# A mixture-of-experts stage that keeps a list of tokens: steps gather by token and add into a sum in DRAM

## The chip, the cores and the metric

One core of one Trainium2 chip. The time is the device time of one launch, in microseconds. Names used below: PE is TensorE, DVE is VectorE, ACT is ScalarE, POOL is GpSimd, SP is SyncE. SP and ACT can issue plain DMAs; POOL issues the indirect ones (rows picked by a list of indices).

## What is computed

Cross-attention followed by a feed-forward layer of eight experts, each token going to two of them, everything in float32. Only the second half is touched by the change:

```python
def _L0_ffn_ref(hidden_states, router_w, w1, w2):
    flat = hidden_states.reshape(-1, H)                    # 1792 tokens x 256
    gate_probs = jax.nn.softmax(flat @ router_w, axis=-1)  # 8 experts
    topk_w, topk_idx = jax.lax.top_k(gate_probs, 2)
    topk_w = topk_w / jnp.clip(topk_w.sum(-1, keepdims=True), EPS)
    cw = jnp.zeros((T, E)).at[jnp.arange(T)[:, None], topk_idx].add(topk_w)
    h = jax.nn.silu(jnp.einsum('td,edf->etf', flat, w1))   # 256 -> 512
    y = jnp.einsum('etf,efd->etd', h, w2)                  # 512 -> 256
    out = jnp.einsum('etd,te->td', y, cw)
...
x = x + _L0_xattn_ref(_layernorm(x), ctx_1024, ctx_1024, mask, Wq, bq, Wk, bk, Wv, bv, Wo, bo)
x = x + _L0_ffn_ref(_layernorm(x), router_w, w1, w2)
```

## The kernel before

The attention half runs over 16 batches and ends near 316 us of the span. Then comes the routing: PE projects the attention output (`project_output`), DVE adds it to `x2` (`residual`, line 972), normalises the rows into `xn2` (`normalise_rows`, line 1006), PE makes the logits, DVE finds each token's first and second expert (`find_first`, `find_second`) and PE ranks the tokens of each expert (`rank`, line 1425).

The experts' work is cut into 21 steps (`STEPS`) of 256 rows (`TG`), each step with the weights of one expert. `place_rows` (line 1052) works out for each token and each of its two choices the row it takes in an array that is sorted by expert. The rows themselves are moved:

- SP fills the DRAM array `sorted_x` (5376 x 256) with zeros (line 416), so that rows that belong to no token are harmless.
- POOL scatters the normalised rows into it: 28 indirect DMAs of 128 rows of 1 KB (line 583), 14 tiles of tokens by two choices.
- In each step SP loads 256 consecutive rows of `sorted_x` (`load_block`, line 438) and two weights of 512 KB (`load_w1`, `load_w2`).
- After step 21, POOL gathers the outputs from `sorted_y` back to the tokens' order, 28 indirect DMAs again (line 610), DVE multiplies each by its weight and adds it to `x2` (line 1169), and SP writes `out` in seven parts (line 469).

Every product is made of three: each operand is split into a high part (a cast to float32r) and a low part (what the cast left over). In step t of the loop the engines do, in this order and all double-buffered (`par`):

- PE (`step`, line 1472): `hidden(t)`, 24 products; `rows_transpose(t+1)`, 4 transposes; `expert_out(t-1)`, 24 products.
- ACT (line 777): high part of w1 of t+1 (`w1_high`), the DMA of the output block t-2 to `sorted_y` (`write_block`), high part of the rows t+1 (`rows_high`), and two Silu passes of t (`silu`: the value and its high part).
- DVE (`expert_step`, line 1119): low part of the rows t+1 (`rows_low`), low part of the hidden values of t (`h_low`), copy of the output t-1 out of PSUM (`copy_y`), high part of w2 of t+1 (`w2_high`).
- POOL (line 591): low parts of w1 of t+1 and of w2 of t (`split_low`).

Steps 0 to 2 and 19 and 20 are written out, those between run in a loop of two steps a turn (`Fori`). The order is that of the program; nothing reorders it. A wait on a semaphore holds all that stands behind it on the same engine.

## Time and profile before

| | |
|---|---|
| runs, us | 590.64, 589.96, 587.99; median 589.96 |
| the profiled execution, us | 589.78, its span 588.0 |
| busy: PE, DVE, ACT, POOL | 435.2, 376.6, 231.5, 264.1 us |
| granted TensorE clock, mean over the span | 0.877 |
| attention with its start | 0 to 316 us |
| output projection, routing, ranking | 316 to 363 us |
| POOL's scatter of the rows | 363 to 400 us |
| first row block to last output | 400 to 544 us |
| gather, weighted sum, write | 545 to 588 us |

The span runs from the first to the last instruction of the profiled execution; 1.8 us of its own time lie around it. The stages are read off the timelines and the chain that ended last. A matmul's row lasts longer than the distance to the next one, since they are pipelined: distances between starts are the measure. Indirect DMAs stand under POOL with the time in which POOL makes them; their landing is a different number, in the view of the DMA issues.

### The profile page before, as it was taken

Reading aid. Unit: us, or ns where it says so; the run is one execution under the profiler, and the core shown is the slowest. Engines: PE = TensorE matmul, PEld = TensorE weight load, DVE = VectorE, ACT = ScalarE, POOL = GpSimd, SP = SyncE. Lnnn points to the kernel's source line nnn. Section 1 sums busy time; section 2 is a strip of 40 time slices with the busy share of each in tenths; the row PEclk is TensorE's granted clock in tenths of the full one; section 3 lists DMA queues with packets and bytes.
Section 4 is the critical chain, followed back from the end, with each engine's and each line's share of the span. In section 5 each row is a group of like instructions: output and inputs, shape, how many; then the busy total and the mean of one; then the engine's idle time right before and its main releaser. Section 6 shows DMA issues by size and latency. Waiting matters only on the chain.

```text
span 588.0 us, 10921 instructions
## 1 busy us (share of the span) xinstructions
PE 435.2 (74%) x4123; PEld 384.7 (65%) x4123; DVE 376.6 (64%) x749; ACT 231.5 (39%) x296; POOL 264.1 (45%) x170
## 2 busy tenths in 40 slices
PE   2657799999999999999987482004999999998000
PEld 2546588888888888878766472003999999998000
DVE  3765647777777777777734856001899999997233
ACT  3321245555555555555552030001645554552000
POOL 7352412222221122222004202775699899895574
PEclk9886679999999999999998775555999999999655
DMA  7979499999899998997443700525588787862354
GB/s 190 182 192 256 151 136 142 139 130 141 142 139 144 143 140 142 141 142 104 48 129 118 258 1 33 200 107 180 165 261 245 243 258 233 254 213 90 107 155 130
DMA packets 82025, 93.00 MB, mean 158 GB/s; under 512 B 19345, under 2 KB 74801, under 8 KB 81985
## 3 DMA queue, kind: packets, MB, share of 16 engines
q1 hardware_dynamic: 73584, 79.60, 63.1%
q0 software_dynamic: 2688, 7.34, 4.0%
q10 hardware_dynamic: 5712, 5.51, 2.8%
q8 instruction: 27, 0.44, 0.4%
q14 instruction: 14, 0.11, 0.1%
HBM read 51.58 MB, written 22.14 MB: 125 GB/s over the span
## 4 chain that ended last, share of the span: by engine, by line
PE 44%; issue 16%; DVE 16%; POOL 9%; ACT 8%; DMA 3%; ACTq 2%; DVEq 0%; POOLq 0%; SPq 0%
PE ps L1182 17%; PE ps L1232 9%; PE ps L1248 7%; PE ps L1262 5%; POOL sorted_x L583 4%; POOL chosen_rows L610 4%; DVE neg_max L839 4%; ACT h_hi L771 3%; ACT h_f L770 2%; DVE y_out L1116 2%; DVE k_f L823 2%; ACTq L775 1%; PE ps L1275 1%; DVE h_lo L1109 1%; ACT probs L660 1%
## 5 line engine op out<-in xcount | busy, mean ns | idle before, releaser
L839 DVE TENSOR_REDUCE neg_max<-ps 112x1 f32<-112x376 f32 x256 | 133.0, 546 | 48.1 <-PE ps L1232 44.4
L588 POOL TENSOR_TENSOR w_lo<-w_raw,w_hi 128x1024 fp32r<-128x1024 f32 x42 | 117.8, 2826 | 24.0 <-DVE w_hi L1105 14.3
L660 ACT ACTIVATE probs<-ps 125x1344 f32<-125x1344 f32 x64 | 82.8, 1293 | 59.0 <-PE ps L1248 56.3
L1232 PE MATMUL ps<-k_stack,q_stack 98*112 98x376 f32 x256 | 90.5, 396 | 10.3 <-issue 5.2
L498 POOL TENSOR_TENSOR k_lo<-k_f,k_hi 128x752 fp32r<-128x752 f32 x16 | 28.7, 1791 | 87.4 <-ACT k_hi L634 84.8
L489 POOL TENSOR_TENSOR ctx_lo<-ctx_raw,ctx_hi 128x752 fp32r<-128x752 f32 x16 | 28.8, 1798 | 80.3 <-ACT ctx_hi L627 80.3
L1232 PEld LDWEIGHTS ps<-k_stack,q_stack 98*112 98x112 f32 x256 | 43.0, 182 | 27.5 <-DVE neg_max L839 21.3
L1109 DVE TENSOR_TENSOR h_lo<-h_f,h_hi 128x1024 fp32r<-128x1024 f32 x21 | 52.6, 2503 | 11.1 <-ACT h_hi L771 11.1
L1248 PE MATMUL ps<-q_stack,k_stack 100*125 100x224 f32 x384 | 54.8, 279 | 2.1 <-ACT probs L660 2.1
L1248 PEld LDWEIGHTS ps<-q_stack,k_stack 100*125 100x125 f32 x384 | 51.2, 193 | 2.8 <-ACT probs L660 1.8
L1182 PE MATMUL ps<-flat_t_hi,w_hi 128*128 128x256 f32 x168 | 50.4, 300 | 3.3 <-DVE flat_t_lo L1098 3.2
L1262 PE MATMUL ps<-probs,v_wide 125*32 125x112 f32 x1536 | 50.2, 264 | 0.7 <-ACT probs L660 0.7
L1182 PE MATMUL ps<-w_hi,h_hi 128*128 128x256 f32 x168 | 49.2, 293 | 1.9 <-DVE h_lo L1109 1.9
L754 ACT CAST flat_t_hi<-ps 128x512 fp32r<-128x512 f32 x21 | 12.3, 587 | 94.5 <-PE ps L1443 94.5
L1182 PE MATMUL ps<-flat_t_hi,w_lo 128*128 128x256 f32 x168 | 48.1, 286 | 0.0
L1182 PE MATMUL ps<-flat_t_lo,w_hi 128*128 128x256 f32 x168 | 48.0, 286 | 0.0
L1182 PE MATMUL ps<-w_lo,h_hi 128*128 128x256 f32 x168 | 47.4, 282 | 0.0
L1182 PE MATMUL ps<-w_hi,h_lo 128*128 128x256 f32 x168 | 47.4, 282 | 0.0
L583 POOL DMA_INDIRECT sorted_x<-xn,place x28 | 27.2, 971 | 44.5 <-DVE place L1071 36.3
L1443 PE MATMUL ps<-ident,rows 128*128 128x128 f32 x84 | 13.1, 280 | 43.6 <-DMA rows<-sorted_x 43.6
L1105 DVE CAST w_hi<-w_raw 128x1024 fp32r<-128x1024 f32 x21 | 45.3, 2156 | 0.0
L1262 PEld LDWEIGHTS ps<-probs,v_wide 125*32 125x32 f32 x1536 | 34.8, 110 | 13.2 <-issue 11.8
(169 smaller groups left out, 990.0 us busy)
## 6 DMA issues: line engine op xcount, KB each, us to landing
w_raw<-w SPq DMA_DIRECT2D x42, 512.0 KB, 3.8
k_stack<-k_hi SPq DMA_DIRECT2D x64, 188.0 KB, 6.1
k_stack<-k_lo SPq DMA_DIRECT2D x32, 188.0 KB, 8.9
ctx_raw<-ctx_t SPq DMA_DIRECT2D x32, 187.5 KB, 8.3
q_stack<-q_scratch SPq DMA_DIRECT2D x32, 168.0 KB
sorted_x<-zeros SPq DMA_DIRECT2D x1, 5376.0 KB, 17.5
rows<-sorted_x SPq DMA_DIRECT2D x21, 256.0 KB, 3.9
sorted_y<-y_out ACTq DMA_DIRECT2D x21, 256.0 KB, 2.9
```

The costliest lines, as they stand in the source:

```text
L489: pool.tensor_tensor(cl[b.par][:, :, :], c_raw[b.par][:, :, :], ch[b.par][:, :, :].bitcast(F32), ALU.subtract).then_inc(cl_ready, 1)
L498: pool.tensor_tensor(kl[:, :, :], kf[:, :, :], kh[:, :, :].bitcast(F32), ALU.subtract)\
L583: pool.indirect_dma_start(sorted_x, bass.IndirectOffsetOnAxis(ap=place[c][:, n:n + 1], axis=0), xn2[:, n, :], None).then_inc(scattered, 16)
L588: pool.tensor_tensor(low[t.par][:, :, :], raw[:, :, :], high[t.par][:, :, :].bitcast(F32), ALU.subtract).then_inc(done, 1)
L660: act.activation(pf[j % 2][:, :, :], ps[0:CT, BK_ST:BK_ST + KT, 0:4 * S], ACT.Exp).then_inc(pf_ready, 1)
L839: dve.tensor_reduce(neg_max[:, s:s + 1], ps[0:S, BK_MAX + s % 2, 0:CP], AX.X, ALU.max, negate=True).then_inc(max_read, 1)
L1105: dve.tensor_copy(w2h[t.par][:, :, :], w_raw[t.par][1][:, :, :]).then_inc(w2h_ready, 1)
L1109: dve.tensor_tensor(hl[t.par][:, :, :], hf[t.par][:, :, :], hh[t.par][:, :, :].bitcast(F32), ALU.subtract).then_inc(hl_ready, 1)
L1182: last = pe.matmul(o, lhs, rhs, start=n == 0, stop=n == len(terms) - 1)
L1232: pe.matmul(ps[0:S, BK_MAX + a, 0:CP], qs[b.ring][0:R_MAX, q, S * a:S * (a + 1)], ks[b.ring][0:R_MAX, q, :], start=True, stop=True).then_i ...
L1248: last = pe.matmul(ps[0:CT, BK_ST + k3, 2 * S * q:2 * S * (q + 1)], ks[b.ring][0:ROWS, 2 * j + q, k3 * CT:(k3 + 1) * CT], qs[b.ring][0:ROW ...
L1262: last = pe.matmul(ps[VC * i:VC * (i + 1), BK_OUT, S * j:S * (j + 1)], vx[b.par][:, k3, 2 * j + i // 2 + HALF * (i % 2), :], pf[j % 2][:, ...
```

## The change

Not the rows are sorted, but a list of pairs (token, weight). What it does, by engine; line numbers of the changed kernel are those of this section only:

- **The list.** POOL makes two small tables early on: `no_row` (pairs for rows that belong to no token: the token number is T..T+255, a spare row, and the weight 0) and the token numbers of `of_token` (lines 555 to 558). SP writes `no_row` to `sorted_rows` (5376 x 2) during the first turn of the attention. `weigh` stands ahead of `place_rows` on DVE, and puts the weights into `of_token`. POOL then scatters the pairs, 28 indirect DMAs of 128 pairs of 8 bytes. SP loads the list back (`load_rows_of`, line 452): the pairs of steps 0 and 1 first, then those of the 19 others, each step with two pairs a partition.
- **Inputs.** SP writes `xn2` to `xn_rows` and `x2` to `total`, seven parts each, with 256 spare rows of zeros. The zero fill of `sorted_x` is gone.
- **Steps.** POOL gathers the rows of step t+2 by token, two indirect DMAs (`gather_rows`, line 599), and then adds the output of step t-1 into `total`, two indirect DMAs with an addition (`add_rows`, line 611). Each `add_rows` waits until the one before has landed. No step is written by ACT, and none loaded by SP.
- **Weights.** The low parts of w1 and w2 go from POOL to DVE, the high part of w2 from DVE to ACT (`w2_high`, line 787). DVE multiplies the output by the weight of its row as it takes it out of PSUM (`weigh_y`, line 1124), two instructions of 128 x 256 in place of one copy of 128 x 512.
- **End.** The gather, the weighted sum on DVE and the seven writes are gone. SP waits for the last addition and copies `total` to `out`, DRAM to DRAM, in one DMA of 1792 KB.
- All 21 steps are written out on every engine, without a loop. Two mask tables of the attention share space with `probs`.

```diff
@@ gpsimd @@
+            pool.memset(no_row[:, :, :, 1], 0.0)
+            pool.iota(no_row[:, :, :, 0].bitcast(I32), pattern=[[0, STEPS], [1, 2]], base=T, channel_multiplier=2)\
+                .then_inc(tokens_set, 1)
...
             pool.wait_ge(placed, 1)
-            pool.wait_ge(zero_rows, 16)
+            pool.wait_ge(weights_ready, 1)
+            pool.wait_ge(rows_cleared, 16)
             for n in range(NT):
                 for c in range(TOP):
-                    pool.indirect_dma_start(sorted_x, bass.IndirectOffsetOnAxis(ap=place[c][:, n:n + 1], axis=0),
-                                            xn2[:, n, :], None).then_inc(scattered, 16)
+                    pool.indirect_dma_start(sorted_rows, bass.IndirectOffsetOnAxis(ap=place[c][:, n:n + 1], axis=0),
+                                            of_token[:, n, c, :], None).then_inc(scattered, 16)
+            def token_of(t, a):
+                return bass.IndirectOffsetOnAxis(ap=of_row[:, t.n, a, 0:1].bitcast(I32), axis=0)
+            def gather_rows(t):
+                if t.n == 0:
+                    pool.wait_ge(xn_written, 16 * (NTG + 1))
+                    pool.wait_ge(of_row_in[0], 16)
+                if t.n == FIRST_STEPS:
+                    pool.wait_ge(of_row_in[1], 16)
+                if not early(t, 2):
+                    pool.wait_ge(rt_done, t.n - 1)
+                for a in range(2):
+                    pool.indirect_dma_start(rows[t.par][:, a, :], None, xn_rows, token_of(t, a))\
+                        .then_inc(rows_in[t.par], 16)
+            def add_rows(t):
+                pool.wait_ge(y_copied, 2 * (t.n + 1))
+                if early(t, 1):
+                    pool.wait_ge(total_written, 16 * (NTG + 1))
+                else:
+                    pool.wait_ge(y_added, 16 * 2 * t.n)
+                for a in range(2):
+                    pool.indirect_dma_start(total, token_of(t, a), yo[t.par][:, a, :], None, compute_op=ALU.add)\
+                        .then_inc(y_added, 16)
+            for n in range(-2, STEPS + 1):
+                t = Batch(0, n)
+                if is_step(t.after(2)):
+                    gather_rows(t.after(2))
+                if is_step(t.after(-1)):
+                    add_rows(t.after(-1))
@@ sync @@
-                sp.dma_start(rows[t.par][:, :, :], block_rows(sorted_x, t))\
-                    .then_inc(rows_in[t.par], 16)
+            def load_rows_of(steps, done):
+                sp.dma_start(of_row[:, steps, :, :],
+                             sorted_rows[TG * steps.start:TG * steps.stop, :]
+                             .rearrange("(s p n) c -> p s n c", p=P, n=2)).then_inc(done, 16)
...
+            sp.wait_ge(y_added, 16 * 2 * STEPS)
+            sp.dma_start(out, total[0:T, :].rearrange("(n p) d -> n p d", p=P)).then_inc(out_written, 16)
@@ scalar @@
-            def write_block(t):
-                act.wait_ge(y_copied, t.n + 1)
-                act.dma_start(block_rows(sorted_y, t), yo[t.par][:, :, :]).then_inc(y_written[t.par], 16)
+            def w2_high(t):
+                act.wait_ge(w2_in[t.par], 16 * (t.turn + 1))
...
                 if is_step(t):
                     silu(t)
+                    w2_high(t)
@@ vector @@
-            def copy_y(t):
...
+            def weigh_y(t):
                 dve.wait_ge(y_done, t.n + 1)
                 if not early(t, 2):
-                    dve.wait_ge(y_written[t.par], 16 * t.turn)
+                    dve.wait_ge(y_added, 16 * 2 * (t.n - 1))
+                for a in range(2):
+                    dve.tensor_scalar(yo[t.par][:, a, :], ps[:, BK_Y + t.par, D * a:D * (a + 1)],
+                                      of_row[:, t.n, a, 1:2], None, ALU.mult).then_inc(y_copied, 1)
             def expert_step(t):
+                after = t.after(1)
+                if is_step(after):
+                    split_low(after, w_raw[after.par][0], w1h, w1l, w1h_ready, w1l_ready)
+                    rows_low(after)
+                if is_step(t.after(-1)):
+                    weigh_y(t.after(-1))
                 if is_step(t):
                     h_low(t)
+                    split_low(t, w_raw[t.par][1], w2h, w2l, w2h_ready, w2l_ready)
```

DVE in one turn of the loop before (`flat_t_lo` is the rows' low part, `h_lo` the hidden values', `w_hi` is w2's high part):

```order
L1098 TENSOR_TENSOR flat_t_lo_123<-ps,flat_t_hi_121 128x512
L1108 REGISTER_ALU
L1109 TENSOR_TENSOR h_lo_120<-h_f_116,h_hi_118 128x1024
L1113 REGISTER_ALU
L1115 ISA
L1116 COPY y_out_127<-ps 128x512
L1102 ISA
L1105 CAST w_hi_75<-w_raw_68 128x1024
```

DVE in one step of the changed kernel (`w_lo_178` belongs to w1, `w_lo_78` to w2):

```order
L1116 TENSOR_TENSOR w_lo_178<-w_raw_175,w_hi_177 128x1024
L1111 TENSOR_TENSOR flat_t_lo_126<-ps,flat_t_hi_124 128x512
L1129 TENSOR_SCALAR y_out_130<-ps,token_and_weight_of_row 128x256 x2
L1121 TENSOR_TENSOR h_lo_121<-h_f_117,h_hi_119 128x1024
L1116 TENSOR_TENSOR w_lo_78<-w_raw_70,w_hi_77 128x1024
```

Two low parts of weights came to DVE and one high part left it; the output is now taken out ahead of `h_lo`, where it was behind it.

POOL in the steps of the changed kernel, where it had only `split_low` before:

```order
L608 DMA rows_127<-xn_rows,token_and_weight_of_row 128x256 x2
L618 DMA total<-y_out_130,token_and_weight_of_row 2048x256 x2
L608 DMA rows_128<-xn_rows,token_and_weight_of_row 128x256 x2
L618 DMA total<-y_out_129,token_and_weight_of_row 2048x256 x2
L608 DMA rows_127<-xn_rows,token_and_weight_of_row 128x256 x2
```

The gathers of a later step stand ahead of the additions of an earlier one in POOL's queue, so the two alternate.

## Rows read from the trace of the kernel before

**Rows 1.** Windows of the stretch: us, busy us of each engine, clock, DMA share, GB/s

```profile
core 0: us, PE busy (x) PEld busy (x) DVE busy (x) ACT busy (x) POOL busy (x), PEclk, DMA share, GB/s
363.40:366.90 3.50, 0.00 (x0) 0.00 (x0) 3.12 (x13) 0.00 (x0) 2.59 (x4) 0.50 0.23 65
425.00:540.00 115.00, 114.40 (x936) 111.72 (x934) 106.43 (x73) 59.55 (x71) 101.94 (x36) 1.00 0.75 228
545.00:588.00 43.00, 0.00 (x0) 0.00 (x0) 13.63 (x29) 0.00 (x0) 26.75 (x28) 0.54 0.46 134
```

**Rows 2.** Chain that ended last: start us, us, what it consists of

```profile
362.81 1.20 POOL sorted_x L583
...
397.27 2.40 DMA sorted_x<-xn,place
399.69 2.83 DMA rows<-sorted_x
402.56 1.13 PE ps L1443 x4
...
541.22 3.15 PE ps L1182 x24
...
581.54 2.88 DMA chosen_rows<-sorted_y,place
```

**Rows 3.** Timeline of POOL and DVE in the expert loop: start us, us, operation

```profile
488.38 5.73 POOL L588 TENSOR_TENSOR w_lo<-w_raw,w_hi 128x1024 fp32r<-128x1024 f32 x2 [0.63 <-DVE w_hi L1105]
...
489.28 2.56 DVE L1109 TENSOR_TENSOR h_lo<-h_f,h_hi 128x1024 fp32r<-128x1024 f32 x1 [0.38 <-ACT h_hi L771]
491.77 0.68 DVE L1116 COPY y_out<-ps 128x512 f32<-128x512 f32 x1
492.37 2.28 DVE L1105 CAST w_hi<-w_raw 128x1024 fp32r<-128x1024 f32 x1
```

**Rows 4.** Timeline of PE over one expert step late in the loop

```profile
527.14 0.39 PE L1182 MATMUL ps<-flat_t_hi,w_hi 128*128 128x256 f32 x1
...
530.08 0.60 PE L1443 MATMUL ps<-ident,rows 128*128 128x128 f32 x4
530.44 0.36 PE L1182 MATMUL ps<-w_hi,h_hi 128*128 128x256 f32 x1
...
533.28 0.28 PE L1182 MATMUL ps<-w_hi,h_lo 128*128 128x256 f32 x1
533.51 0.39 PE L1182 MATMUL ps<-flat_t_hi,w_hi 128*128 128x256 f32 x1
```

**Rows 5.** Timeline of DVE while POOL was between two of its operations

```profile
414.26 1.23 DVE L1109 TENSOR_TENSOR h_lo<-h_f,h_hi 128x1024 fp32r<-128x1024 f32 x1 [2.56 <-ACT h_hi L771]
```

**Rows 6.** Lines: durations ns min/median/max, first and last start, shapes

```profile
L868 DVE TENSOR_TENSOR attn_rows<-ps,rsum x16: 424/424/425, 100.6 to 314.2; 112x256 f32<-112x256 f32 x16
...
L761 ACT CAST w_hi<-w_raw x21: 1044/1059/1066, 368.7 to 527.3; 128x1024 fp32r<-128x1024 f32 x21
...
L610 POOL DMA_INDIRECT chosen_rows<-sorted_y,place x28: 942/949/1087, 547.5 to 581.5; - x28
L1169 DVE SCALAR_TENSOR_TENSOR x<-chosen_rows,weight,x x28: 483/484/485, 551.6 to 585.0; 128x256 f32<-128x256 f32 x28
```

**Rows 7.** DMA issues: KB each, median us from issue to landing

```profile
sorted_x<-zeros SPq DMA_DIRECT2D x1, 5376.0 KB, 17.5
rows<-sorted_x SPq DMA_DIRECT2D x21, 256.0 KB, 3.9
...
x<-x_tiles SPq DMA_DIRECT2D x1, 1792.0 KB, 7.8
...
sorted_x<-xn,place POOLq DMA_INDIRECT x28, 2.4
chosen_rows<-sorted_y,place POOLq DMA_INDIRECT x28, 2.8
```

**Rows 8.** Timeline of DVE at the ranking: idle time before it in brackets

```profile
359.11 0.17 DVE L1055 COPY counts<-ps 128x8 f32<-128x8 f32 x1 [3.59 <-PE ps L1433]
```

More of the change, by code:

```diff
@@ L591, in step @@
-            def step(t):
-                after = t.after(1)
-                if is_step(after):
-                    split_low(after, w_raw[after.par][0], w1h, w1l, w1h_ready, w1l_ready)
-                if is_step(t):
-                    split_low(t, w_raw[t.par][1], w2h, w2l, w2h_ready, w2l_ready)
-            for n in range(-1, 3):
-                step(Batch(0, n))
-            with pool.Fori(0, LOOP_STEPS) as i:
-                for off in (3, 4):
-                    step(Batch(i, off))
@@ L1091, in weigh @@
                 step(dve.tensor_tensor(cw[:, :, :], t1[:, :, :], wide2(c0), ALU.mult))
-                for one_of, w in ((picked, weight[0]), (second, weight[1])):
+                for c, one_of in enumerate((picked, second)):
                     step(dve.tensor_tensor(t0[:, :, :], cw[:, :, :], one_of[:, :, :], ALU.mult))
-                    step(dve.tensor_reduce(w[:, :], t0[:, :, :], AX.X, ALU.add))
+                    last = dve.tensor_reduce(of_token[:, :, c, 1], t0[:, :, :], AX.X, ALU.add)
+                    if c + 1 < TOP:
+                        step(last)
+                last.then_inc(weights_ready, 1)
             def rows_low(t):
@@ L1495, in _ @@
             rank()
-            for n in range(-1, 3):
-                step(Batch(0, n))
-            with pe.Fori(0, LOOP_STEPS) as i:
-                for off in (3, 4):
-                    step(Batch(i, off))
-            for n in range(3 + 2 * LOOP_STEPS, STEPS + 1):
+            for n in range(-1, STEPS + 1):
                 step(Batch(0, n))
```

150 lines of the change are left out of this document (57 added, 93 removed).

## The prediction, made before the changed kernel ran

> **What bounds the kernel now.** I began with the windows of the stretches [rows 1], since a share of the span tells nothing of a kernel with such unlike stages. In the middle row, 425 to 540 us, PE is busy for 114.4 of 115 us at the full clock (2.4 GHz): the expert steps are bound by PE. In the last row, 545 to 588 us, PE and ACT do nothing, DVE 13.6 us, and POOL 26.75 us: here the kernel waits for POOL to make the 28 gathers. The chain of waits [rows 2] says the same of the start of the steps: POOL's scatter begins at 362.81, its last DMA is issued at 397.27 and lands in 2.40, the load of the first block takes 2.83, and PE transposes at 402.56. So two stretches of about 40 us lie around the steps in which POOL issues DMAs. Each of them costs POOL about 0.95 us [rows 6], and from start to start it is (581.5 - 547.5) / 27 = 1.26 us; in the scatter (397.27 - 362.81) / 27 = 1.28.
>
> Then I looked at how tight the steps are. PE's hidden product starts at 527.14 and the next one at 533.51: 6.37 us, of which nothing is idle [rows 4]. DVE is nearly as full: 2.56 + 0.68 + 2.28 and 0.68 for the rows' low part, the same shape as the copy, make 6.20 us, but two of these are stretched by POOL, whose two subtractions run for 5.73 us beside them [rows 3]. With POOL between two operations the same `h_lo` took 1.23 us [rows 5].
>
> **The scatter stays.** 28 indirect DMAs of 128 elements go to 28 of 128 elements; the elements shrink from 1 KB to 8 bytes. Nothing shows that the issue depends on the bytes: I take 1.28 us each and a landing of 2.4 as before, so 36.9 us, no change. Bounds: it might fall if bytes mattered, and 28 times 0.1 us would be 2.8 either way. `weigh` now stands ahead of `place_rows`: 12 instructions, DVE busy for about 3.1 us of a 3.5 us window [rows 1]. DVE sat idle there for 3.59 us until PE had ranked [rows 8], so PE's ranking hides it, at most 0.2 us late. If that cover were gone, it would cost its 3.7 us.
>
> **The start of the steps gets longer.** Before: load of a block, 2.83 us. Now: SP loads the first part of the list, then POOL makes two gathers, then these land. The list's load I price at 2.4 us (the landing of the scatter; above it is bounded by the 3.9 of a block's load in traffic [rows 7], and no row bounds it below, so I go a third down, to 1.6); the gathers are 1.26 + 2.8 [rows 7]. The sum 6.5 less 2.83 is +3.7. The second part of the list is 19 steps in pieces of 16 bytes, issued right behind the first and ahead of the gathers in time; I add 1.0 for what it takes from them (0 to 4). `expert_out(0)` waited for `h_lo` before; now w2's low part comes behind `h_lo` on DVE, one more operation of 1.23 [rows 5]: +1.2. Together **+5.9**.
>
> **The steps.** PE's own work is unchanged, 6.37 us. POOL per step: four DMAs at 1.26 to 1.28, 5.1 us, below 6.37. An addition waits for the one before to land, but between the two stand the gathers' 2.5 us; 1.26 + 2.8 and another 1.1 for traffic (3.9 against 2.83 [rows 2, 7]) is 5.2, again below. ACT: it had 59.55 us of work in 115 us, 3.3 a step, and gets a cast of 1.06 [rows 1, 6]: 4.4. DVE per step without POOL's subtractions: three operations of 1.23, 0.68, and two of 0.42 (a product of 112 x 256 out of PSUM [rows 6]): 5.2 us, less the overlaps of some 0.08. By sums nobody is late.
>
> By order it is closer. DVE takes out y(t-1) ahead of `h_lo` and w2's low part of t, and `expert_out(t)` needs both. From the end of `expert_out(t-1)`, 533.28 + 0.28 = 533.56, to the next `expert_out` PE has a hidden product and four transposes to do. The hidden product starts at 533.51, and with its transposes takes 530.44 - 527.14 = 3.30 [rows 4], so the next `expert_out` could start at 536.81, 3.25 after the end of the last. DVE needs 0.76 for the two products, 1.15 and 1.23 for the two subtractions, and about 0.1 for the semaphores: **3.24**. So the cover is used up to the last tenth, and every slowdown of DVE in this place is paid in full, 20 times. I take 0.08 us a step, **+1.6**. The low bound is 0 (PE's 6.37 is a floor). For the upper bound DVE's work beside POOL's DMAs must be priced: the weighted sums in the last stretch, with two inputs in SBUF, ran beside POOL's gathers at 483 to 485 ns, all 28 of them [rows 6], and POOL kept its 1.26. That is the nearest row, and it shows no contention; I allow 0.3 a step, +6.
>
> Here the Trainium skill speaks against the change. "SBUF — State Buffer", section "Who interferes with whom", says that a DVE instruction with two SBUF inputs contends with a GpSimd instruction that reads SBUF, and that the one that starts second is blocked whole. By that, if making a DMA counts as reading, the sum would be that of the third rival. For POOL's subtractions the trace agrees (2.56 against 1.23).
>
> The loads of SP are issued when the low parts are ready, w1's more than 5 us ahead of the next cast, while a block's load in the same traffic lands in 3.9 us [rows 7], and SP has lost these block loads: 0. That the loop is written out is worth at most the 0.6 us in 115 in which PE was idle [rows 1]: 0.
>
> **The last step.** `expert_out(20)` started at 541.22 [rows 2], held by `h_lo`; now y(19) goes first and w2's low part behind, the output before ends at about 539.5, and 539.5 + 3.24 = 542.7: **+1.5**.
>
> **The end.** Before: from the last output, 541.22 + 3.15 = 544.37, to 588.0: 43.6 us. Now: weighing 0.8, first addition's start to the second's 1.26, landing 2.4 (as the scatter, also a write to DRAM) and the copy of 1792 KB. The nearest row for that is the load of the same 1792 KB from DRAM into SBUF, 7.8 us [rows 7]. Below it is bounded by the fill's rate, 17.5 x 1792 / 5376 = 5.8, above by twice 7.8 = 15.6, if reading and writing DRAM don't overlap. I take 7.8, and 0.3 for the waits: 12.6. So **-31.0**. The addition has no row: 2.4 from below, twice a gather's landing, 5.6, from above.
>
> What SP writes in addition in the routing (two times seven parts of 256 KB) takes the place of the fill of 5376 KB, 17.5 us; nothing waits for it before 400 us: 0. The clearing of the list in the first turn of the attention is 2688 pieces of 16 bytes, and POOL makes its tables there, behind which SP and POOL stand; PE bounds that stage, and loads run ahead: 0, at most 3.
>
> **Sum** against the profiled execution, 589.78: +5.9 + 1.6 + 1.5 - 31.0 = -22.0, so **567.8 us**. The median of the runs is 0.2 above it, which I leave out. With all low bounds (start +3.5, steps 0, end -33.0 with the 5.8 us copy, last step +1) it is 561; with the high ones (start +10, steps +6, copy and addition dear, -20, the rest +2) it is 588.
>
> **Rivals.**
>
> *A. Adding in DRAM is dear.* The engine must read before it writes, and the next addition waits for the last. If from the start of one pair's first DMA to its landing it takes 7.0 us instead of 5.2, or POOL needs 1.9 us instead of 0.95 to make one (then 2 x 1.26 + 2 x 2.2 = 6.9), POOL sets the step at about 7.0: 20 x 0.6 = +12, and +2 at the end: **582 us**. For it: no row shows such a DMA. Against: 1.2 us of slack. "Collectives: The Full Stack", of the Trainium skill, section "The bandwidth ceiling", says that an addition in a DMA costs no time by itself but needs two source reads, each with its descriptor; no run here shows it. By that, making one would cost 0.95 x 1.5 = 1.4 as an estimate, a step of 6.0 for POOL, and no change of the sum.
>
> *B. DVE's path is stretched in part.* With 0.5 us a step more than the cover: 20 x 0.5 = +10, less the 1.6 in the sum: **576 us**. For it: the slack is 0.01 by my count. Against: the 28 even rows.
>
> *C. POOL's DMAs hold DVE as its subtractions did: slower.* If making an indirect DMA holds up DVE's subtractions as POOL's did, `h_lo` and w2's low part on the tight path go from 1.23 to 2.56 each: +2.7 a step, 20 steps, +53: **620 us**. It turns slower than before from (22.0 + 1.6) / 20 = 1.2 us a step on. For it: `h_lo` at 2.56 beside POOL [rows 3]. Against: [rows 6], the same kind of DMA beside DVE operations with two SBUF inputs.
>
> *D. The gain is larger,* because the 8-byte scatter is quicker or the copy near its lower bound: **559 us**.
>
> **Chances.** The forecast, 561 to 575: 0.64. A 0.14, B 0.10, C 0.08, D 0.04. A difference of 0.5% (2.9 us) is about what a measurement here can tell from none. Of A and B 0.04 reaches into that band; C alone is slower. So faster 0.88, same 0.04, slower 0.08. The range, 559 to 585, takes in A and B at their prices and leaves out C and the edges.
>
> **What would show it.** Right: 28 DMAs of the scatter at 1.28; PE's transposes at 406 to 408; hidden products 6.37 to 6.5 apart; DVE's subtractions at 1.23; from the last output to the end 12 to 14 us, of which the copy 8. Wrong: subtractions over 1.4 (B, C); POOL without idle time, or an addition that lands later than 4 us (A); a copy of 12 us or more; PE idle ahead of `expert_out`, with w2's low part as releaser, for more than 0.3.

## The result and the profile after

The changed kernel takes **607.63 us** (median of 4 runs, 606.35 to 608.47) against 589.52 for the kernel before beside it: ratio 1.031, 95% interval 1.028 to 1.033. It is slower, and the 567.8 us forecast, its range and its direction are wrong. The profiled execution has a span of 606.5 us, 18.5 more than before.

The windows first: the steps, then the stretch that [rows 1] shows with POOL alone at work.

```profile
core 0: us, PE busy (x) PEld busy (x) DVE busy (x) ACT busy (x) POOL busy (x), PEclk, DMA share, GB/s
434.00:580.00 146.00, 123.80 (x927) 120.42 (x926) 87.30 (x108) 75.80 (x88) 108.39 (x70) 0.92 0.73 186
545.00:588.00 43.00, 33.37 (x246) 32.24 (x245) 24.21 (x30) 19.14 (x22) 29.71 (x19) 0.91 0.58 135
```

In the steps PE is idle for 15% of the time, where [rows 1] had it full. POOL is busy for 108.4 of 146 us, and at least 0.3 us stands between any two of its DMAs: 70 x 0.3 = 21 more. The gathers and additions of the steps, by line (columns: line, engine, operation, count | busy us, mean ns | idle before, and what ended it):

```profile
L618 POOL DMA_INDIRECT total<-y_out,token_and_weight_of_row x36 | 68.0, 1889 | 27.6 <-DMA total<-y_out,token_and_weight_of_row 13.7 <-issue 9.6 <-DVE y_out L1129 4.2
L1116 DVE TENSOR_TENSOR w_lo<-w_raw,w_hi 128x1024 fp32r<-128x1024 f32 x36 | 42.4, 1217 | 0.0
L608 POOL DMA_INDIRECT rows<-xn_rows,token_and_weight_of_row x34 | 41.6, 1225 | 10.4 <-issue 10.4
L1121 DVE TENSOR_TENSOR h_lo<-h_f,h_hi 128x1024 fp32r<-128x1024 f32 x18 | 21.8, 1214 | 0.0
```

DVE's subtractions take 1.21 to 1.22 us, as in [rows 5]: nothing holds DVE. It is POOL whose work is long: 1.89 and 1.22 us for one DMA, where [rows 6] had 0.95. The timelines of POOL and DVE show when (start us, us, operation):

```profile
480.35 1.94 POOL L618 DMA_INDIRECT total<-y_out,token_and_weight_of_row  x1 [0.38 <-issue]
482.59 1.92 POOL L618 DMA_INDIRECT total<-y_out,token_and_weight_of_row  x1 [0.30 <-issue]
484.82 1.01 POOL L608 DMA_INDIRECT rows<-xn_rows,token_and_weight_of_row  x1 [0.31 <-issue]
486.13 1.99 POOL L608 DMA_INDIRECT rows<-xn_rows,token_and_weight_of_row  x1 [0.30 <-issue]
490.38 1.62 POOL L618 DMA_INDIRECT total<-y_out,token_and_weight_of_row  x1 [2.26 <-DMA total<-y_out,token_and_weight_of_row]
...
495.51 1.23 POOL L608 DMA_INDIRECT rows<-xn_rows,token_and_weight_of_row  x1 [0.30 <-issue]
```

```profile
479.58 1.21 DVE L1121 TENSOR_TENSOR h_lo<-h_f,h_hi 128x1024 fp32r<-128x1024 f32 x1
480.71 2.35 DVE L1116 TENSOR_TENSOR w_lo<-w_raw,w_hi 128x1024 fp32r<-128x1024 f32 x2
...
486.05 1.21 DVE L1121 TENSOR_TENSOR h_lo<-h_f,h_hi 128x1024 fp32r<-128x1024 f32 x1
487.18 2.35 DVE L1116 TENSOR_TENSOR w_lo<-w_raw,w_hi 128x1024 fp32r<-128x1024 f32 x2
...
494.65 1.22 DVE L1121 TENSOR_TENSOR h_lo<-h_f,h_hi 128x1024 fp32r<-128x1024 f32 x1
```

The gather of 486.13 starts just after `h_lo` has begun; `w_lo` follows at 487.18, so 1.05 us of `h_lo` were left, and 1.05 + 0.95 = 2.00 us is what the gather took (1.99). That of 495.51 starts 0.28 before the next `w_lo` (495.79): 0.28 + 0.95 = 1.23. The addition of 480.35: 0.36 to the end of `h_lo`, and 1.94 in all, which leaves 1.58. So a DMA that starts inside a subtraction is longer by what was left of that one, and the subtraction behind it adds nothing. This holds, to 0.1 us, for all 29 DMAs that start inside a subtraction between the third `h_f` and the last; the 41 others take 0.98 to 1.01 us (gathers) and 1.57 to 1.62 (additions). And an addition takes 1.55 to 1.62 us where nothing holds it (1.55 at 594.83, with DVE idle).

The other new thing is in the chain of waits, with the start, a stretch of the steps and the end (start us, us, what):

```profile
399.90 2.71 DMA sorted_rows<-token_and_weight,place
402.63 2.31 DMA token_and_weight_of_row<-sorted_rows
404.98 0.74 issue
405.72 0.98 POOL rows L608
...
407.01 4.46 DMA rows<-xn_rows,token_and_weight_of_row
411.52 1.13 PE ps L1442 x4
...
482.59 7.02 DMA total<-y_out,token_and_weight_of_row
...
489.65 0.73 issue
490.38 1.62 POOL total L618
...
592.74 1.78 POOLq L79
594.52 0.30 issue
594.83 1.55 POOL total L618
```

An addition lands up to 7.0 us after its start, and the next one begins 0.77 us after that landing. Here is where the 18.5 us come from, with the start of `h_f` on ACT as the mark of a step:

| stretch | before, us | after, us | difference | forecast |
|---|---|---|---|---|
| to the scatter's first DMA | 362.8 | 365.4 | +2.6 | 0 |
| from there to the first `h_f` | 49.5 | 56.9 | +7.4 | +4.7 |
| first to third `h_f` | 11.2 | 11.4 | +0.2 | +1.2 |
| 18 periods (6.34; now 8.15) | 114.1 | 146.7 | **+32.6** | +1.4 |
| last `h_f` to the last y taken out | 7.5 | 12.3 | +4.8 | +1.5 |
| from there to the end | 42.9 | 13.8 | -29.1 | -31.0 |

The end brought what was expected of it (28 DMAs gone, the copy landing in 7.4 us where 7.8 was taken). The steps took it back and more. The first row is no firm difference: in the profiled executions of experiments that leave the attention as it is in the changed kernel, the scatter begins anywhere from 362 to 372 us. What lies behind the scatter doesn't carry that variation, and it took 225.2 us before and 241.1 after.

### The profile page after: what moved, and what is told of

Its sections match the earlier page's. It is cut to its first block, busy times and chain, and to the rows that moved or that the text cites. A ratio compares the mean times of both kernels' runs of the same rounds, so it can differ in the third digit from the quotient of the medians.

```text
span 606.5 us, 10628 instructions
## 1 busy us (share of the span) xinstructions
PE 449.2 (74%) x4123; PEld 396.6 (65%) x4123; DVE 345.3 (57%) x763; ACT 250.9 (41%) x317; POOL 248.1 (41%) x187
## 4 chain that ended last, share of the span: by engine, by line
PE 42%; POOL 17%; DVE 13%; DMA 12%; issue 10%; ACT 3%; POOLq 0%; SPq 0%
PE ps L1181 17%; DMA total<-y_out,token_and_weight_of_row 9%; POOL total L618 9%; PE ps L1231 9%; PE ps L1247 7%; PE ps L1261 5%; POOL sorted_rows L593 4%; DVE neg_max L848 4%; POOL rows L608 3%; DVE k_f L832 2%; DMA rows<-xn_rows,token_and_weight_of_row 1%; PE ps L1274 1%; DVE x_rows_sb L901 1%; ACT probs L674 1%; PE ps L1403 1%
## 5 line engine op out<-in xcount | busy, mean ns | idle before, releaser
L618 POOL DMA_INDIRECT total<-y_out,token_and_weight_of_row x42 | 78.2, 1863 | 43.3 <-DMA total<-y_out,token_and_weight_of_row 16.6
L1442 PE MATMUL ps<-ident,rows 128*128 128x128 f32 x84 | 14.9, 305 | 72.0 <-DMA rows<-xn_rows,token_and_weight_of_row 71.8
L1231 PEld LDWEIGHTS ps<-k_stack,q_stack 98*112 98x112 f32 x256 | 43.5, 185 | 30.4 <-DVE neg_max L848 21.8
L608 POOL DMA_INDIRECT rows<-xn_rows,token_and_weight_of_row x42 | 49.9, 1189 | 24.0 <-issue 11.9
L768 ACT CAST flat_t_hi<-ps 128x512 fp32r<-128x512 f32 x21 | 12.3, 588 | 113.8 <-PE ps L1442 113.8
L1442 PEld LDWEIGHTS ps<-ident,rows 128*128 128x128 f32 x84 | 9.9, 150 | 74.9 <-DMA rows<-xn_rows,token_and_weight_of_row 74.7
L1181 PE MATMUL ps<-w_hi,h_hi 128*128 128x256 f32 x168 | 54.8, 326 | 5.2 <-issue 3.7
L1116 DVE TENSOR_TENSOR w_lo<-w_raw,w_hi 128x1024 fp32r<-128x1024 f32 x42 | 49.6, 1218 | 9.0 <-ACT w_hi L775 9.0
L1181 PE MATMUL ps<-w_lo,h_hi 128*128 128x256 f32 x168 | 52.8, 314 | 0.0
L1181 PE MATMUL ps<-w_hi,h_lo 128*128 128x256 f32 x168 | 52.7, 314 | 0.0
L1181 PE MATMUL ps<-flat_t_hi,w_hi 128*128 128x256 f32 x168 | 48.7, 290 | 2.8 <-DVE flat_t_lo L1111 2.8
L1111 DVE TENSOR_TENSOR flat_t_lo<-ps,flat_t_hi 128x512 fp32r<-128x512 f32 x21 | 14.5, 689 | 63.7 <-ACT flat_t_hi L768 63.7
```

Of the source, the lines that this page charges most:

```text
L608: pool.indirect_dma_start(rows[t.par][:, a, :], None, xn_rows, token_of(t, a))\
L618: pool.indirect_dma_start(total, token_of(t, a), yo[t.par][:, a, :], None, compute_op=ALU.add)\
L1116: dve.tensor_tensor(low[t.par][:, :, :], raw[:, :, :], high[t.par][:, :, :].bitcast(F32), ALU.subtract).then_inc(done, 1)
L1181: last = pe.matmul(o, lhs, rhs, start=n == 0, stop=n == len(terms) - 1)
L1231: pe.matmul(ps[0:S, BK_MAX + a, 0:CP], qs[b.ring][0:R_MAX, q, S * a:S * (a + 1)], ks[b.ring][0:R_MAX, q, :], start=True, stop=True).then_i ...
L1442: last = pe.transpose(ps[:, BK_T + t.par, TG * k + P * a:TG * k + P * (a + 1)], rows[t.par][:, a, k * P:(k + 1) * P], ident[:, :])
```

## The experiments

Each ran beside the kernel before on the same chip; ratios are to it. "Period" is the distance of two `h_f` starts, mean of the 18 from the third to the last, in the profiled execution.

**1. No addition, only the write** (the sum in DRAM is left out of the result: rows overwrite each other).

```
-  pool.indirect_dma_start(total, token_of(t, a), yo[t.par][:, a, :], None, compute_op=ALU.add)
+  pool.indirect_dma_start(total, token_of(t, a), yo[t.par][:, a, :], None)
```

> The changed kernel with the addition in the DMA left out: add_rows writes its rows to total instead of adding them (so each token keeps only the output of the step that wrote last, without its residual). Waits, order and bytes are unchanged. Theories of the steps' 8.1 us (before: 6.37): L, the addition lands late (about 7 us after its issue) and the next must wait for it; P, POOL needs too long to issue (1.6 to 2.6 us for an addition, 0.95 for a gather); D, DVE's path to the next output product is stretched. L and P both expect quicker steps here, 6.4 to 6.7 us, and 571 to 580 us in all; D expects steps of about 8 and over 600 us. The issue of a write should fall to 0.95 us by P; if it stays at 1.6, the cost is in the scatter to DRAM and not in the addition.

594.93 us, ratio 1.007 (1.004 to 1.010), period 7.41: between the two. A plain write takes 0.98 to 1.0 us to make where nothing holds it, and up to 2.0 where a subtraction does: the long ones stay. Its landings still order the writes, as its chain of waits shows:

```profile
481.90 6.83 DMA total<-y_out,token_and_weight_of_row
...
488.77 0.73 issue
489.50 1.00 POOL total L618
```

**2. Two sums in turn**: even steps add into one, odd ones into another that the output leaves out, so no addition waits for the step before.

```
+  y_added = [sem(f"y_added{p}") for p in range(2)]
-      pool.wait_ge(y_added, 16 * 2 * t.n)
+      pool.wait_ge(y_added[t.par], 16 * 2 * t.turn)
-      pool.indirect_dma_start(total, ...)
+      pool.indirect_dma_start((total, total_odd)[t.par], ...)
```

> The changed kernel with two sums in DRAM, even steps adding into one and odd steps into the other, so that an addition waits for the one before last only. The odd sum is left out of the output; both get x2 first. Number, size and kind of the additions are unchanged. L: the wait for the landing is gone, steps of 6.4 to 6.8 us, 575 to 583 us. P: POOL is busy or between two issues for 0.88 of the steps' time as it is, so the steps fall to about 7.2 us only, 586 to 592 us. If the landings themselves stretch (the DMA engines can do no more additions), steps stay at 8, over 600.

610.14 us, ratio 1.036 (1.031 to 1.041), period 8.06. Without the landing nothing is won, so POOL's queue must be as long as the chain of landings:

```profile
478.73 1.91 POOL L612 DMA_INDIRECT rows<-xn_rows,token_and_weight_of_row  x1 [0.31 <-issue]
480.95 2.60 POOL L622 DMA_INDIRECT total<-y_out,token_and_weight_of_row  x1 [0.30 <-issue]
483.85 1.58 POOL L622 DMA_INDIRECT total<-y_out,token_and_weight_of_row  x1 [0.30 <-issue]
485.73 1.01 POOL L612 DMA_INDIRECT rows<-xn_rows,token_and_weight_of_row  x1 [0.30 <-issue]
487.05 1.88 POOL L612 DMA_INDIRECT rows<-xn_rows,token_and_weight_of_row  x1 [0.30 <-issue]
```

This is POOL's timeline: it goes from one to the next without a wait for anybody. Over the steps an addition takes 2.11 us to make and a gather 1.26, so 2 x 2.11 + 2 x 1.26 + 4 x 0.3 = 7.9 of the 8.06 us are POOL's queue. So the third case of the expectation, landings that stretch, isn't needed to explain the 8.06.

**3. Small weights**: from the third step on, only a part of w1 and w2 is loaded (the rest of the raw tiles is old data).

```
+  few = slice(0, None if early(t, 2) else 1)
-  sp.dma_start(w_raw[t.par][part][:, :, :], w[bass.ds(e, 1), :, :, :]...)
+  sp.dma_start(w_raw[t.par][part][:, few, :], w[bass.ds(e, 1), few, :, :]...)
```

> The changed kernel with the weights' loads cut from step 2 on to one part (w1 to a half, w2 to a quarter), so 1 MB a step becomes 384 KB and the output is not the reference's. It asks why an addition lands 7 us after its issue when the last two, at the end and without traffic, landed in 3.7. If traffic of the weights is the reason, the landings fall to 4 to 5 us, and the steps to 6.5 to 7.2: 575 to 590 us. If it is the gathers queued behind, or the addition as such, landings stay at 6 to 7 and the time over 600.

603.75 us (one run), period 8.06. The traffic falls from 195 to 113 GB/s (440 to 560 us), and four of the five additions on the chain land in 3.6 us instead of 5 to 7, the fifth in 6.1. The step stays: traffic makes landings late, but isn't what bounds. POOL's queue is full here as in 2 (2 x 2.08 + 2 x 1.28 + 4 x 0.3 = 7.9 us), since more of its DMAs now start inside a subtraction.

**4. The low parts alone**: the kernel before, with the subtractions moved from POOL to DVE and w2's cast to ACT, in the changed kernel's order; the rest as before.

```
-  pool.tensor_tensor(low[t.par][:, :, :], raw[:, :, :], high..., ALU.subtract)
+  dve.tensor_tensor(low[t.par][:, :, :], raw[:, :, :], high..., ALU.subtract)
-  dve.tensor_copy(w2h[t.par][:, :, :], w_raw[t.par][1][:, :, :])
+  act.copy(w2h[t.par][:, :, :], w_raw[t.par][1][:, :, :])
```

> The kernel before with one part of the change alone: low parts of w1 and w2 on DVE, high part of w2 on ACT, the output's copy ahead of h_lo; scatter, loads, sorted_y and the last gather as before, and the loop kept. The prediction's count (3.24 us of DVE work under 3.25 of cover) expects steps of 6.37 to 6.5 us and 588 to 592 us, DVE's subtractions at 1.22. D expects steps over 6.8 and over 598 us.

593.81 us, ratio 1.0065 (1.003 to 1.010), period 6.26. This part holds in the steps: DVE's path of 3.24 us against a cover of 3.25 doesn't tear. (The copy of y takes 0.1 us less to the next start than the changed kernel's two products; experiment 11 has those, and a period of 6.30.) What it costs is at the last step, in the chain:

```profile
537.79 3.10 PE ps L1169 x24
...
541.52 1.23 DVE h_lo L1095
542.74 1.23 issue
543.97 4.63 PE ps L1169 x24
```

PE stands for 3.1 us while DVE does y(19), `h_lo` and w2's low part in a row, and then the same 24 products take 4.63 us, where [rows 2] had 3.15.

After these four the theory was: making an indirect DMA on POOL waits for the DVE subtraction under way (two inputs in SBUF), and this, not the landing, fills POOL's queue.

**5. The subtractions read PSUM** instead of SBUF as their first input, in the changed kernel. What they compute are then no low parts, and PE's hidden product waits for them besides, so as not to overwrite the banks that they read.

```
-  dve.tensor_tensor(low[t.par][:, :, :], raw[:, :, :], high..., ALU.subtract)
+  dve.tensor_tensor(low[t.par][:, :, :], ps[:, 2 * t.par:2 * t.par + 2, :]..., high..., ALU.subtract)
```

> All three subtractions of a step on DVE (w1, w2 and h low parts) take their first input from PSUM banks instead of SBUF, so their values aren't the low parts; everything else is as in the changed kernel. Theory P (making an indirect DMA on POOL waits whole while a DVE operation with two SBUF inputs is under way, about 1.0 us each, two a step): additions 1.55 to 1.62 us each to make at line 618 without a second size near 2.6, gathers 0.95 to 1.0 at line 608, POOL 2x1.6 + 2x0.95 + 4x0.3 = 6.3 a step, the period back at 6.4 to 6.9, 575 to 582 us. Rival Q (the long ones wait for something of their own, as memory or the ring of descriptors): 607 as before, sizes stay at 1.6 and 2.6. DVE's operations should last the 1.2 us they last now under both.

598.31 us, ratio 1.017 (1.013 to 1.022), period 7.54. By line, 440 to 560 us:

```profile
L618 POOL DMA_INDIRECT total<-y_out,token_and_weight_of_row x31 | 49.6, 1601 | 28.8 <-DMA total<-y_out,token_and_weight_of_row 23.3 <-issue 5.5
L1117 DVE TENSOR_TENSOR w_lo<-ps,w_hi 128x1024 fp32r<-128x1024 f32 x31 | 36.4, 1216 | 0.0
L608 POOL DMA_INDIRECT rows<-xn_rows,token_and_weight_of_row x32 | 31.9, 998 | 9.8 <-issue 9.8
```

The mechanism is shown: not one DMA is held any more (between 440 and 550 us every addition 1.57 to 1.63, every gather 0.98 to 1.01), and DVE's operations last what they lasted. The size was wrong: the step doesn't go to 6.4, since POOL now waits for landings.

**6. Both edits**: the two sums of 2, and the subtractions from PSUM of 5.

> The same edit on top of the kernel with two sums (odd steps add into a sum of their own, which is left out of the output, so that no addition waits for the landing of the step before). If a chain of landings (make 3.1, land 2.5 to 3, weigh) still holds the step once POOL is free, this is 5 to 10 us faster than the kernel with the low parts from PSUM alone; if not, the two are within 3 us, both 575 to 582.

595.86 us, ratio 1.011 (1.008 to 1.014), period 7.34: neither 575 nor much better than 5. Something third was there. From the timelines of POOL, and of PE's transposes:

```profile
474.63 1.62 POOL L622 DMA_INDIRECT total<-y_out,token_and_weight_of_row  x1 [1.17 <-DVE y_out L1135]
476.56 1.58 POOL L622 DMA_INDIRECT total<-y_out,token_and_weight_of_row  x1 [0.31 <-issue]
478.44 1.01 POOL L612 DMA_INDIRECT rows<-xn_rows,token_and_weight_of_row  x1 [0.30 <-issue]
479.75 0.99 POOL L612 DMA_INDIRECT rows<-xn_rows,token_and_weight_of_row  x1 [0.30 <-issue]
```

```profile
485.12 0.66 PE L1448 MATMUL ps<-ident,rows 128*128 128x128 f32 x4 [2.06 <-DMA rows<-xn_rows,token_and_weight_of_row]
```

The gathers stand behind the additions, and these behind the weighing of y at 473.48. They land 5.1 us (median) after their start, 484.9, and PE has waited 2.06 us for them. Behind the transposes comes the output product, whose y is weighed at 488.68, two steps after that of 473.48: a ring of weighing, additions, gathers, landing, transposes and output product of 15.2 us, 7.6 a step.

**7. The clearing of `sorted_rows` after the attention**, not in its first turn.

```
+  sp.wait_ge(tokens_set, 2)
+  sp.dma_start(sorted_rows..., no_row...).then_inc(rows_cleared, 16)
   sp.wait_ge(tri_set, 1)
   for rows_of, done in ((xn_rows, xn_written), (total, total_written)):
```

> The clearing of sorted_rows (43 KB in pieces of 16 bytes) is issued after the attention instead of at 87 us of it; nothing else changes. If its small pieces hold the loads and heads beside it, the attention gets back 1 to 3 us (the h-scores of batch 1 at 104.3 instead of 106.8, the output projection at 317 to 319 instead of 320.3) and the time is 604 to 606; if the lateness of the attention is from elsewhere, 607.6 with the same 320.3. The clearing must be done by 365, and nothing then waits for it.

604.62 us, ratio 1.024 (1.022 to 1.027), against 1.031 (1.028 to 1.033) for the changed kernel: 3 to 4 us. From the scatter to the end both take 241.1 us, so it lies ahead of the scatter. But the output projection, at 316.49 before and 320.30 after, starts at 317.23 here and at 315.49 in experiment 13, which clears as early as the changed kernel does. The time says that the clearing costs something; single profiles don't carry it, and whether it is the small pieces that cost is not shown.

**8. Rows in the scatter, parts instead of a sum.** The scatter moves whole rows as before, each with its place and weight behind it (1032 bytes); SP loads blocks; POOL only writes the weighted outputs, each row to a place of its own (token and choice); at the end SP loads both parts, DVE adds.

```
-  sorted_rows, xn_rows, total
+  sorted_x = nc.dram_tensor("sorted_x", [STEPS * TG, D + 2], F32).ap()
+  parts = nc.dram_tensor("parts", [TOP * T + 2 * TG, D], F32).ap()
+      pool.indirect_dma_start(parts, token_of(t, a), yo[t.par][:, a, :], None)
```

> The scatter carries whole rows as in the kernel before, with the row's place in the parts and its weight behind the 256 values (1032 bytes); SP loads each step's rows as one plain block; POOL only writes the two blocks of weighted outputs of a step, each row to a place of its own (token and choice), so nothing is read, added or ordered; at the end SP loads both parts, DVE adds them to x2 and seven pairs are written out; low parts on DVE. Theory P: POOL has 2 x 0.95 to 2.0 + 0.6 a step = at most 4.6 of 6.4, never the bound, so the period is 6.3 to 6.4; scatter as before or +0.1 each (1032 bytes), start as in the kernel before, end 0.8 + 1.0 + 0.3 + 2.4 + 2 x 4 (14 loads) + 1 + 3 = 15 after the last product against 43.6: 563 to 572 us, faster than both. If the writes of outputs themselves (not their addition) are what holds the steps, the period stays over 7 and the time over 580.

601.36 us, ratio 1.021 (1.017 to 1.025), period 7.60, so neither the 6.3 to 6.4 nor the time of the expectation. POOL has slack there (65 of 140 us busy, and it waits for y), but with four row buffers the load of a block waits for the writes of two steps before, and the weights' load stands behind it in SP's queue.

**9. Gathers first**: POOL makes those of the step after next ahead of the additions.

```
-  for n in range(-2, STEPS + 1):     gather_rows(t.after(2))
+  for n in range(-3, STEPS + 1):     gather_rows(t.after(3))
```

> POOL makes the gathers of the step after next ahead of the additions (the order of the loop alone; the values are the same). Theory P+L: two things hold the steps: POOL's queue (two DMAs of a step held by a DVE operation each, 2x1.6 + 2x0.95 + 4x0.3 + about 2.0 = 8.2), and a loop weigh, additions, gathers, landing, transposes, weigh. In the changed kernel the first is the longer, so the order alone gives little: period 7.8 to 8.2, 600 to 608 us. If the loop alone were the bound, the period would be 6.4 and the time 573.

615.73 us, ratio 1.043 (1.040 to 1.046): slower than the changed kernel, which no theory had. The profiled execution took 621.6 us, since its attention was 5 us longer than the changed kernel's (the output projection starts at 325.29, against 320.30). Only about one DMA a step is held now, mostly by 0.4, and the period is 8.30 all the same. The chain of waits in its steps is made of landings:

```profile
488.53 1.62 POOL total L618
490.15 0.30 issue
490.46 5.84 DMA total<-y_out,token_and_weight_of_row
```

1.62 + 0.30 + 5.84 and 0.77 to the next addition's start are 8.5 us. The same chain is in the changed kernel, beside the full queue, but there it passes through a landing in 8 of 18 steps, here in 16. And here DVE stands for the landing too, since the weighing must not overwrite a buffer whose addition hasn't landed:

```profile
496.40 0.88 DVE L1129 TENSOR_SCALAR y_out<-ps,token_and_weight_of_row 128x256 f32<-128x256 f32 x2 [3.66 <-DMA total<-y_out,token_and_weight_of_row]
497.19 1.22 DVE L1121 TENSOR_TENSOR h_lo<-h_f,h_hi 128x1024 fp32r<-128x1024 f32 x1
```

The landing was at 496.30, `h_lo` stands behind the weighing, and POOL's second addition (499.00) falls into the subtractions each time. From the scatter to the end this kernel takes 248.4 us, 7.3 more than the changed one: 2.7 are in the 18 periods, most of the rest behind the last `h_f` (31.4 us to the end, against 26.1).

**10. Gathers first, subtractions from PSUM**: the edits of 9 and 5.

> The same order with the three subtractions reading PSUM (values wrong, as in that kernel before). Theory P+L: both holds are gone, POOL 6.3 a step, period 6.3 to 6.6, and the time 573 to 580 us, against 598 with the subtractions from PSUM alone. If it stays at 7.3 to 7.5, the loop isn't what holds that kernel.

585.43 us, ratio 0.993 (0.990 to 0.996), period 6.75. Two of the three are out, and it is faster than before. The miss of 5 us is the landings again: 3.6 to 6.0 us on the chain, and 11 us of waits for them in 116.

**11. Six row buffers** in the kernel of 8, so that a load waits for older writes.

```
-  BLOCKS = 4
+  BLOCKS = 6
-  sp.wait_ge(y_written[t.par], 32 * (t.turn - 1))
+  sp.wait_ge(y_written[t.par], 32 * (t.turn + 1 - BLOCKS // 2))
```

> The kernel with whole scattered rows and parts, with six row buffers instead of four (the load of a block waits for the writes of four steps before the last, not two; in the kernel with four it was issued at 497.04, when the writes made at 488.7 and 490.7 had landed, and the load of the weights stood behind it). With that wait gone: period 6.3 to 6.5, last h_f at 539 to 543, 568 to 576 us. If the period stays over 7, POOL's writes of outputs are themselves the cost.

**575.22 us, ratio 0.978** (0.974 to 0.982), with nothing left out of the result, period 6.30. POOL's writes are held there too (1.69 and 1.97 us), and it costs nothing, since POOL has two DMAs a step and not four (window of 430 to 540 us, columns as in the first view):

```profile
430.00:540.00 110.00, 109.03 (x898) 105.79 (x898) 82.87 (x102) 74.65 (x87) 63.00 (x35) 1.00 0.68 233
```

**12. A shorter end** for it: in the last step `h_lo` and w2's low part ahead of the weighing of y(19), and half of the parts' loads issued by ACT.

```
-  if is_step(t.after(-1)):
+  if is_step(t.after(-1)) and t.n != STEPS - 1:
       weigh_y(t.after(-1))
   ...
+  if t.n == STEPS - 1:
+      weigh_y(t.after(-1))
```

> The kernel with six buffers and parts (575 us), with a shorter end: in the last step DVE makes the low parts of h and w2 ahead of weighing y(19), and ACT issues the loads of the second part beside SP's of the first (14 issues of 0.5 us stood in a row there). Expected: last y weighed at 546 to 547.5 instead of 548.9, the loads issued in 3.6 us instead of 7.9, together 4 to 6 us less: 569 to 571 us. If the loads are bound by their transfer (3.6 MB at some 300 GB/s) and not by their issue, only 1 to 3 us: 572 to 574.

572.25 us, ratio 0.970 (0.966 to 0.973), the fastest of all. From the last `h_f` to the start of the last weighing it is 7.6 us against 11.3. From its end to the end of the kernel it is 21.8 against 22.7: a second engine that issues brought 0.9 us, so the loads were bound by their transfer and not by their issue. Experiments 11 and 12 beat both kernels.

**13. Two sums, gathers first** (the edits of 2 and 9): what DVE's hold on POOL costs alone.

> The changed kernel with two sums (odd steps' additions left out of the output) and the gathers first: neither the landing of the last addition nor the place of the gathers behind additions can hold a step; what is left is POOL's queue with DVE's subtractions holding it. By the gathers-first kernels one or two DMAs a step are held by 0.4 to 1.0: 2x1.6 + 2x1.0 + 4x0.3 + 0.4 to 2.0 = 6.8 to 8.4. Expected by theory P: a period of 7.0 to 8.0 and 585 to 605 us. If it comes to 6.4 and 575, the holding of POOL costs nothing by itself and the landings were all.

591.64 us, ratio 1.005 (1.002 to 1.008), period 7.01, as theory P had it.

**14. All three out**: the edits of 2, 5 and 9.

> The same with the subtractions reading PSUM: all three holds are out. Theory: POOL 6.35 a step against PE's 6.37, period 6.35 to 6.5 from the third step on, with POOL nearly full, PE hardly idle, 572 to 578 us; that would be 5 to 10 us above the prediction of 567.8, the rest being start, attention and end. If the period stays over 6.7, something of the changed kernel is not found yet.

576.38 us, ratio 0.979 (0.974 to 0.985), period 6.33. PE is full again, and POOL nearly so: 87.2 + 67 x 0.3 = 107 of 110 us (window of 430 to 540 us).

```profile
430.00:540.00 110.00, 109.99 (x900) 106.78 (x899) 84.52 (x105) 73.51 (x86) 87.19 (x67) 1.00 0.93 244
```

The eight combinations:

| held by DVE | landings in a row | gathers behind additions | period, us | scatter to end, us | time, us |
|---|---|---|---|---|---|
| yes | yes | yes | 8.15 | 241.1 | 607.6 (changed kernel) |
| no | yes | yes | 7.54 | 229.8 | 598.3 (5) |
| yes | no | yes | 8.06 | 239.7 | 610.1 (2) |
| yes | yes | no | 8.30 | 248.4 | 615.7 (9) |
| no | no | yes | 7.34 | 227.1 | 595.9 (6) |
| no | yes | no | 6.75 | 217.1 | 585.4 (10) |
| yes | no | no | 7.01 | 221.1 | 591.6 (13) |
| no | no | no | 6.33 | 207.4 | 576.4 (14) |

The period and the stretch from the scatter to the end are of the profiled execution, the time is the median. In experiment 13 the profiled execution, at 584.9 us, was the fastest of ten; its output projection starts 5 us earlier than the changed kernel's, so much of what it lies below the median may be in the attention.

The three together account for the steps' whole loss. No one of them does: each taken out alone gives 9 us or nothing, since the other two are nearly as long. Nor do they hide behind one another: left alone, the ring costs 1.0 us a step (6), DVE's hold 0.7 (13) and the landings 0.4 (10), and all three cost 1.8, more than the dearest. By their order they share work, since an addition that is held lies on the chain of landings and on the ring as well; this is argued, no run takes it apart.

## Why the prediction was wrong

**The steps: "POOL per step: four DMAs at 1.26 to 1.28, 5.1 us, below 6.37".** This step failed first. An addition takes 1.6 us to make, not 0.95. Without any hold POOL needs 2 x 1.6 + 2 x 1.0 + 4 x 0.3 = 6.4 a step, already all of PE's 6.37 (experiment 14). I had priced an operation that no row showed at the row of its neighbour, and put the dearer case into rival A with 0.14. Both halves of A came true (1.6 to 1.9 us to make, up to 7.0 to land), but it took them for alternatives and priced the step at 7.0, 582 us; the hold by DVE and the ring were in no rival, and "slower" had its 0.08 from C alone. The signs that I had set for A are those that appeared, and DVE's subtractions stayed at 1.22, which rules out B and C.

**"It shows no contention."** I read [rows 6] for a hold on DVE, and found none; right, DVE is never held. That the same rows could show a hold on POOL I answered with its 1.26. But in that stretch DVE's sums of rows waited for a gather's landing and mostly started where POOL had begun the next gather. In the kernel before only 8 of the 28 gathers started inside a sum, seven of them with 0.01 to 0.15 us of it left. The eighth had 0.26 left, and it is the maximum of 1087 in [rows 6], which I passed over:

```profile
579.41 1.00 DVE L1169 SCALAR_TENSOR_TENSOR x<-chosen_rows,weight,x 128x256 f32<-128x256 f32 x2 [1.76 <-DMA chosen_rows<-sorted_y,place]
580.15 1.09 POOL L610 DMA_INDIRECT chosen_rows<-sorted_y,place  x1 [0.30 <-issue]
```

The rule of the Trainium skill that I named ("SBUF — State Buffer", "Who interferes with whom": the one that starts second is blocked whole) was the right one, and I worked out only one of its two directions, in rival C. With the other it would have been: POOL's DMAs held by what is left of a subtraction, up to 1.2 us each. The runs agree with the rule on that side (486.13: 1.99 us; experiment 5: none held). The same section infers that a `tensor_tensor` does not stall the generation of descriptors; here it holds up the making of a DMA, and the measurement decides. The runs don't show DVE held by POOL's DMAs, so rival C's mechanism, for which I gave 620 us, is not what happened.

**"1.26 + 2.8 and another 1.1 for traffic is 5.2, again below."** The chain of additions is mostly 1.6 to 1.9 to make the first, 0.3, a landing of 4.9 to 7.0 from the start of the second, and 0.77 until the next starts: 7.6 to 10 us. Experiment 3 says that what a landing takes over 3.6 us goes with the traffic, experiment 1 that a plain write lands little earlier (mostly 5 to 6 us). So what was mis-sized in this chain is first of all the landing, and not because it adds: I took it from a scatter into an idle memory. I also left out 0.77 of a wait on a landing.

**The order of POOL's queue was not followed round.** I checked each engine's sum and each chain inside one step. The ring over two steps (experiment 6) is in none of my terms, though all its pieces stood there: what the order puts behind the waiting addition is the gather of the step after next.

**DVE's tight path: right.** The cover of 3.25 against 3.24 held; experiments 4 and 11 have periods of 6.26 and 6.30. I had spent my doubts (B, C) on the one that was sound.

**The start: +4.7 to the first `h_f`, measured +7.4.** The list's load was 2.31 (forecast 2.4); the gathers' landing 4.46, where I had 2.8 and 1.0 for traffic, and 0.74 until POOL starts was left out. Another 1.1 us lies behind the transposes: the first hidden product ran at 0.50 of the full clock and took 5.49 us, where it had 0.61 and 4.77 before; that the clock rises later was in no term. The +1.2 for w2's low part in the first step measured +0.2.

**The last step: +1.5, measured +4.8**, 4.2 of it already in experiment 4. The wait itself was priced right: PE stands for 3.2 us behind `expert_out(19)`, as the 3.24 said, where it stood for 1.6. Of the rest, 1.5 is the clock, which fell to 0.63, so that the last product took 4.6 us instead of 3.1. And `expert_out(19)` ends 3.5 us after the last `h_f`, where it was 2.0; 0.9 of this is only the mark, since in the kernel before the last `h_f` itself came late, behind ACT's write of an output block (it stood 3.96 us for `y_out`).

**The end: -31.0, measured -29.1**; the copy was right (7.4 us for 7.8). The last two additions start 1.85 us apart, not 1.26 (592.98, in the chain the 1.78 us from 592.74, and 594.83), and the second landed 3.8 us after its start, not 2.4.

**The attention: 0 to 3, measured 2.6 up to the scatter.** That is within what single profiles vary by, and whether the clearing makes it is not settled (experiment 7).

## What to carry to other kernels

Before work is moved onto a queue that is to run beside a full engine, price each operation there twice, alone and started inside its neighbour's longest operation, in both directions; rows in which the two hardly ever start in the disturbing order say little, and their maximum more than their median. Where three limits lie within 10% of each other, taking out one shows nothing: take out all, then put them back one by one. A list of tokens saves the gathers at the end, but puts four DMAs and an ordered sum into each step; a place of its own for each output row keeps the one gain without the other cost, and beat both.

## What the runs showed of the hardware

- Making an indirect DMA on POOL waits for the DVE subtraction of 128x1024 with two SBUF inputs that is under way, to its end, and no further (1.99 against 1.05 + 0.95; 1.23 = 0.28 + 0.95). Such an operation with one PSUM input doesn't hold it (experiment 5: gathers at most 1.01 us, additions at most 1.63), and DVE is not stretched by it (1.21 to 1.28 us in the changed kernel and all experiments). It isn't shown for short operations: in the kernel before a scatter's DMA at 364.31 began beside one of 128x112 with two SBUF inputs (364.27, 0.34 us) and took its usual 0.97.
- An indirect DMA of 128 rows of 1 KB takes 0.95 to 1.0 us to make, one of 128 pairs of 8 bytes 0.96 (the scatter of the changed kernel), an adding one of 1 KB rows 1.55 to 1.64.
- A landing is followed by 0.73 us before POOL starts its next DMA; between two DMAs without a wait it is 0.30.
- After 3.1 us in which PE stood still, the granted clock for the next product was 0.62 (544.0 to 548.5 us of experiment 4), 0.63 in the same place of the changed kernel, against 1.00 before: between its levels of 1.2 and 2.4 GHz, and 4.6 us instead of 3.1 for the same 24 products. In experiment 12, where the gap is 1.0 us, it stayed at 1.00 (549.2 to 552.3 us).
